# A graph network kernel: softmax sums rearranged by GpSimd's transfers, reciprocals of the different denominators only

## The reference

```
ex    = exp(leaky_relu(es[src] + ed[dst]) - max)      # first layer; exp(q.k / sqrt(32)) in the attention
alpha = ex / segment_sum(ex, dst)[dst]
out   = segment_sum(h[src] * alpha[:, :, None], dst)  # 8 heads of 32 columns
x1    = elu(out + b)                                  # first layer only
```

## Time and profile before

| | |
|---|---|
| median of 3 runs | 4061.83 us (4058.06 to 4066.59) |
| the profiled execution | 4059.45 us, its span 4057.7 us |
| first layer's loop, `stage_gat_aggregate` | about 742 to 1613 us of the span |
| attention's loop, `stage_attention` | about 2385 to 3489 us of the span |
| busy over the span | PE 77%, DVE 72%, ACT 56%, GpSimd 3% |
| bytes moved by DMA | 311 MB, mean 77 GB/s |

### The profile page before, as it was taken

How to read it: one execution, slowest core, us unless ns; L and a number is a source line. 1 busy time by engine, 2 the same in 40 slices (tenths; PEclk the granted TensorE clock), 3 DMA queues, 4 the chain that set the end, 5 groups by cost and what they waited for, 6 DMA issues and landing times. The chain is left out here.

```text
span 4057.7 us, 45830 instructions
## 1 busy us (share of the span) xinstructions
PE 3122.0 (77%) x15883; PEld 1597.5 (39%) x15885; DVE 2931.5 (72%) x3369; ACT 2292.0 (56%) x3244; POOL 140.2 (3%) x148
## 2 busy tenths in 40 slices
PE   3024766888888885899499489999999999589587
PEld 2012333322222221788467343333333333367454
DVE  4878987799999997355434649999999999611423
ACT  2000367899999997111133148989898989222032
POOL 0000000000000000000044100000000000000000
PEclk8556998999999998999699789999999999799599
DMA  1000134433333332443322412222222222200000
GB/s 45 0 0 0 71 131 162 123 98 97 98 97 95 97 98 58 150 156 127 121 61 65 151 56 78 76 77 76 76 76 77 76 78 76 77 22 0 14 3 32
DMA packets 178576, 311.21 MB, mean 77 GB/s; under 512 B 25648, under 2 KB 129054, under 8 KB 177880
## 3 DMA queue, kind: packets, MB, share of 16 engines
q1 hardware_dynamic: 172920, 293.84, 23.9%
q0 software_dynamic: 5472, 14.95, 1.2%
HBM read 247.26 MB, written 61.47 MB: 76 GB/s over the span
## 5 line engine op out<-in xcount | busy, mean ns | idle before, releaser
L891 PE MATMUL acc<-weights,messages 128*64 128x400 f32 x3200 | 624.6, 518 | 148.3 <-DVE weights L959 87.1
L2069 PE MATMUL acc<-weights,values 128*64 128x400 f32 x3200 | 639.2, 521 | 13.3 <-DVE weights L2179 9.3
L2176 DVE SCALAR_TENSOR_TENSOR weights<-x,counts 128x1600 f32<-128x1600 f32 x304 | 554.9, 1825 | 33.2 <-ACT x L2145 24.7
L2056 PE MATMUL scores<-q,k 32*128 32x400 f32 x3200 | 388.4, 555 | 71.5 <-ACT x L2140 65.3
L891 PEld LDWEIGHTS acc<-weights,messages 128*64 128x64 f32 x3200 | 202.1, 138 | 567.3 <-DVE weights L959 194.5
L2142 ACT ACTIVATE x<-scores 128x800 f32<-128x800 f32 x496 | 405.1, 838 | 17.2 <-PE scores L2056 17.2
L959 DVE SCALAR_TENSOR_TENSOR weights<-rho,kappa,counts 128x800 f32<-128x800 f32 x400 | 410.0, 1065 | 2.0 <-PE acc L891 2.0
L964 DVE TENSOR_TENSOR weights<-maxima,counts 128x1600 f32<-128x1600 f32 x200 | 363.6, 1818 | 42.4 <-ACT maxima L916 42.4
L911 ACT ACTIVATE maxima<-rho,wx 128x800 f32<-128x800 f32 x400 | 361.7, 952 | 34.6 <-DVE weights L964 30.2
L916 ACT ACTIVATE maxima<-maxima,kappa 128x800 f32<-128x800 f32 x400 | 360.0, 948 | 0.0
L2069 PEld LDWEIGHTS acc<-weights,values 128*64 128x64 f32 x3200 | 196.5, 137 | 407.3 <-issue 254.4
(11 more groups left out here) (311 smaller groups left out, 3647.9 us busy)
## 6 DMA issues: line engine op xcount, KB each, us to landing
counts<-edge_counts SPq DMA_DIRECT2D x200, 400.0 KB, 3.2
counts<-edge_counts SPq DMA_DIRECT2D x400, 200.0 KB, 2.4
edge_counts<-counts_out SPq DMA_DIRECT2D x40, 1000.0 KB, 4.2
counts<-edge_counts SPq DMA_DIRECT2D x25, 1600.0 KB, 7.6
w_first<-in_L_ffn_W_dram SPq DMA_DIRECT2D x8, 512.0 KB, 9.9
w_second<-in_L_ffn_W_dram SPq DMA_DIRECT2D x8, 512.0 KB, 9.6
normed_rows<-normed SPq DMA_DIRECT2D x5, 640.0 KB, 3.9
w_first<-expert_rows SPq DMA_DIRECT2D x5, 640.0 KB, 9.4
```

Source lines behind the costliest of these rows:

```text
L891: ins = nc.tensor.matmul(acc[64 * o:64 * o + 64, p, h, 0:CH], msg[:, t, r % 2 * Q + q, :], w[:, T % WR, q, half(h)], start=(t == 0), stop= ...
L2056: ins = nc.tensor.matmul(sc[:, (n + j // 2) % SR, j % 2, 0:CH], kT[part, r % KF, t * P:(t + 1) * P], q[part, r % 2, :], start=True, stop=True)
L2069: ins = nc.tensor.matmul(acc[64 * e:64 * e + 64, p, 0:CH], msg[:, t, r % KF * 2 + p, D * e:D * e + 2 * D], w[:, U % WR, 2 * p + e, :], sta ...
L2176: ins = nc.vector.scalar_tensor_tensor(out=w[:, U % WR, :, :], in0=out, scalar=EXP_HI, in1=counts, op0=ALU.min, op1=ALU.mult)
```

## The change

Both stages get the same new path, for every round:

- The 8 copies of `stack` on ACT are gone. GpSimd issues transfers instead (`spread_out`): 4 that write one of the 32 equal denominator rows of each head to DRAM, 4 that put the numerators of a head into their rows, and, after the first four have landed, 1 that reads the 4 rows of denominators back, spread over 128 partitions by 25 columns (first layer) or 64 by 25 (attention).
- DVE takes the reciprocal of that small tile only (`invert`; in the attention it is bounded first), behind tile 6 or tile 8 of the next round.
- GpSimd writes it to DRAM (1 transfer) and, after that has landed, reads it back with 4 transfers that repeat each row over 32 partitions (`bring_home`).
- DVE multiplies (`divide`), behind tile 11 or tile 16.
- In the first layer `elu_part` has 3 ACT instructions instead of 5; GpSimd does the other two with one tensor_scalar ahead of its addition.
- `copy_sums` waits for the transfers of the round before, and GpSimd for the tile that it overwrites; ACT no longer waits for that.

The attention's `spread_out` and `bring_home` are those of the first layer with its own offsets and are left out below, as are the lines that call the new functions after the last round.

```diff
 # stage_gat_aggregate
-    SUMS_AT, STACK_AT, DIVIDE_AT, ELU_AT = 0, 2, 10, 17
+    SUMS_AT, INVERT_AT, DIVIDE_AT, ELU_AT = 0, 6, 11, 13
+    SPREAD = CW * Q // P
...
+        spread = core.sb(ctx, "denominators_spread", [P, SPREAD])
+        den_dram = nc.dram_tensor("sums_of_weights", (2, ROUNDS, Q, CW), F32, kind="Internal").ap()
-        less = core.sb(ctx, "minus_one", [P, 1])
...
         def copy_sums(act, r):
+            if r:
+                act.wait_ge(s_raw, r * Q * 16)
+                act.wait_ge(s_stack, r * Q * 16)
             for p in range(2):
                 act.wait_ge(s_used, ((r + 1) * NT - 1) * USED_T + p + 1)
                 nc.scalar.copy(sums[:, p, :].rearrange("p (h n) -> p h n", h=2), acc[:, p, :, 0:CH]).then_inc(s_free, 1)
-            act.wait_ge(s_free, 2 * r + 2)
+
+        def spread_out(pool, r):
+
+            pool.wait_ge(s_free, 2 * r + 2)
+            for q in range(Q):
+                o = 64 * (q % 2) + D
+                pool.dma_start(den_dram[0, r, q:q + 1, :], sums[o:o + 1, q // 2, :]).then_inc(s_raw, 16)
             if r:
-                act.wait_ge(s_y, r)
-
-        def stack(m):
-
-            q = m % Q
-            o = 64 * (q % 2) + D * (m < Q)
-            to = den if m < Q else y
-            nc.scalar.copy(to[D * q:D * q + D, :], sums[o:o + D, q // 2, :]).then_inc(s_den, 1)
-
-        def divide(dve, m, r):
+                pool.wait_ge(s_y, r)
+            for q in range(Q):
+                o = 64 * (q % 2)
+                pool.dma_start(y[D * q:D * q + D, :], sums[o:o + D, q // 2, :]).then_inc(s_stack, 16)
+            pool.wait_ge(s_raw, (r + 1) * Q * 16)
+            pool.dma_start(spread[:, :], den_dram[0, r, :, :].rearrange("q (s n) -> (q s) n", n=SPREAD)).then_inc(s_spread, 16)
+
+        def bring_home(pool, r):
+
+            pool.wait_ge(s_inv, r + 1)
+            pool.dma_start(den_dram[1, r, :, :].rearrange("q (s n) -> (q s) n", n=SPREAD), spread[:, :]).then_inc(s_home, 16)
+            pool.wait_ge(s_home, (r + 1) * 16)
+            for q in range(Q):
+                pool.dma_start(den[D * q:D * q + D, :], den_dram[1, r, q, :].partition_broadcast(D)).then_inc(s_wide, 16)
+
+        def invert(dve, r):
+            dve.wait_ge(s_spread, (r + 1) * 16)
+            nc.vector.reciprocal(spread[:, :], spread[:, :]).then_inc(s_inv, 1)
+
+        def divide(dve, r):
+            dve.wait_ge(s_wide, (r + 1) * Q * 16)
+            dve.wait_ge(s_stack, (r + 1) * Q * 16)
+            nc.vector.tensor_tensor(y[:, :], y[:, :], den[:, :], ALU.mult).then_inc(s_div, 1)
+
+        def elu_part(act, m, r):
 
             if m == 0:
-                dve.wait_ge(s_den, (r + 1) * 2 * Q)
-            if m < 4:
-                part = den[:, m * (CW // 4):(m + 1) * (CW // 4)]
-                nc.vector.reciprocal(part, part).then_inc(s_div, 1)
-            else:
-                dve.wait_ge(s_div, r * 5 + 4)
-                nc.vector.tensor_tensor(y[:, :], y[:, :], den[:, :], ALU.mult).then_inc(s_div, 1)
-
-        def elu_part(act, m, r):
-
-            done = r * 5
-            if m == 0:
-                act.wait_ge(s_div, r * 5 + 5)
+                act.wait_ge(s_div, r + 1)
                 ins = nc.scalar.activation(y[:, :], y[:, :], ACT.Identity, bias=bcol[:, r % 2:r % 2 + 1])
             elif m == 1:
-                act.wait_ge(s_elu, done + 1)
+                act.wait_ge(s_elu, 3 * r + 1)
                 ins = nc.scalar.activation(ey[:, :], y[:, :], ACT.Relu, scale=-1.0)
-            elif m == 2:
-                act.wait_ge(s_elu, done + 2)
-                ins = nc.scalar.activation(y[:, :], y[:, :], ACT.Relu)
-            elif m == 3:
+            else:
+                act.wait_ge(s_elu, 3 * r + 2)
                 ins = nc.scalar.activation(ey[:, :], ey[:, :], ACT.Exp, scale=-1.0)
-            else:
-                act.wait_ge(s_elu, done + 3)
-                ins = nc.scalar.activation(y[:, :], y[:, :], ACT.Identity, bias=less[:, 0:1])
...
             @block.gpsimd
             def _(pool):
                 for r in range(ROUNDS):
-
-                    pool.wait_ge(s_elu, r * 5 + 5)
+                    spread_out(pool, r)
+                    bring_home(pool, r)
+
+                    pool.wait_ge(s_elu, 3 * r + 2)
+                    nc.gpsimd.tensor_scalar(y[:, :], y[:, :], 0.0, -1.0, ALU.max, ALU.add).then_inc(s_upper, 1)
+                    pool.wait_ge(s_upper, r + 1)
+                    pool.wait_ge(s_elu, 3 * r + 3)
                     nc.gpsimd.tensor_tensor(XT[:, r % 2, columns(r):columns(r) + CW], y[:, :], ey[:, :], ALU.add).then_inc(s_y, 1)
...
 # stage_attention
-    PROJECT_AT, SUMS_AT, STACK_AT, DIVIDE_AT = 14, 1, 2, 12
+    PROJECT_AT, SUMS_AT, INVERT_AT, DIVIDE_AT = 14, 1, 8, 16
+    PARTS = 64
+    SPREAD = Q * CH // PARTS
...
         def copy_sums(act, r):
 
             act.wait_ge(s_used, (r + 1) * NT)
+            if r:
+                act.wait_ge(s_raw, r * Q * 16)
+                act.wait_ge(s_stack, r * Q * 16)
             for p in range(2):
                 nc.scalar.copy(sums[:, p, :], acc[:, p, 0:CH]).then_inc(s_free, 1)
-            act.wait_ge(s_free, 2 * r + 2)
...
+        def invert(dve, r):
+
+            dve.wait_ge(s_spread, (r + 1) * 16)
+            nc.vector.tensor_scalar(spread[:, :], spread[:, :], 1e-20, None, ALU.max).then_inc(s_low, 1)
+            dve.wait_ge(s_low, r + 1)
+            nc.vector.reciprocal(spread[:, :], spread[:, :]).then_inc(s_inv, 1)
+
+        def divide(dve, r):
+
+            dve.wait_ge(s_wide, (r + 1) * Q * 16)
+            dve.wait_ge(s_stack, (r + 1) * Q * 16)
+            nc.vector.tensor_tensor(XT[:, r % KF, columns(r)], num, den, ALU.mult).then_inc(s_y, 1)
...
+                        if r and t == INVERT_AT:
+                            invert(dve, r - 1)
+                        if r and t == DIVIDE_AT:
+                            divide(dve, r - 1)
```

More of the change, by code:

```diff
@@ L945, in _ @@
             def _(dve):
-                nc.vector.memset(less[:, :], -1.0).then_inc(s_set, 1)
                 nc.vector.tensor_scalar(nkap[:, :, :], kap[:, :, :], -1.0, None, ALU.mult).then_inc(s_set, 1)
@@ L970, in _ @@
                             bound_rho(r + 1)
-                for m in range(5):
-                    divide(dve, m, ROUNDS - 1)
+                invert(dve, ROUNDS - 1)
+                divide(dve, ROUNDS - 1)
     core.stage_ends()
@@ L2088, in divide, with spread_out @@
-        def divide(dve, m, r):
-            if m == 0:
-                dve.wait_ge(s_den, (r + 1) * 2 * Q)
-                nc.vector.tensor_scalar(den, den, 1e-20, None, ALU.max).then_inc(s_div, 1)
-            elif m < 3:
-                dve.wait_ge(s_div, r * 3 + 1)
-                part = den[:, (m - 1) * (CH // 2):m * (CH // 2)]
-                nc.vector.reciprocal(part, part).then_inc(s_div, 1)
-            else:
-                dve.wait_ge(s_div, r * 3 + 3)
-                nc.vector.tensor_tensor(XT[:, r % KF, columns(r)], num, den, ALU.mult).then_inc(s_y, 1)
+        def spread_out(pool, r):
+            pool.wait_ge(s_free, 2 * r + 2)
+            for j in range(Q):
+                e = j % 2
+                o = 64 * e + D * (1 - e)
+                pool.dma_start(den_dram[0, r, j:j + 1, :], sums[o:o + 1, j // 2, :]).then_inc(s_raw, 16)
+            if r:
+                pool.wait_ge(s_y, r)
+            for j in range(Q):
+                e = j % 2
+                o = 64 * e + D * e
+                pool.dma_start(num[D * j:D * j + D, :], sums[o:o + D, j // 2, :]).then_inc(s_stack, 16)
+            pool.wait_ge(s_raw, (r + 1) * Q * 16)
+            pool.dma_start(spread[:, :], den_dram[0, r, :, :].rearrange("q (s n) -> (q s) n", n=SPREAD)).then_inc(s_spread, 16)
@@ L2149, in _ @@
                         copy_sums(act, r - 1)
-                    if r and 0 <= t - STACK_AT < 2 * Q:
-                        stack(t - STACK_AT)
                 copy_sums(act, ROUNDS - 1)
-                for m in range(2 * Q):
-                    stack(m)
+            @block.gpsimd
+            def _(pool):
+                for r in range(ROUNDS):
+                    spread_out(pool, r)
+                    bring_home(pool, r)
             @block.vector
@@ L2180, in _ @@
                     ins.then_inc(s_w, 1)
-                    if r and 0 <= t - DIVIDE_AT < 4:
-                        divide(dve, t - DIVIDE_AT, r - 1)
-                for m in range(4):
-                    divide(dve, m, ROUNDS - 1)
+                    if r and t == INVERT_AT:
+                        invert(dve, r - 1)
+                    if r and t == DIVIDE_AT:
+                        divide(dve, r - 1)
+                invert(dve, ROUNDS - 1)
+                divide(dve, ROUNDS - 1)
                 dve.wait_ge(s_y, ROUNDS)
```

37 lines of the change are left out of this document (19 added, 18 removed).

## The result

The changed kernel took **3942.12 us** (median of 4 runs, 3937.97 to 3943.77); the kernel before, run beside it, 4060.13. The ratio is 0.9705, with a 95% interval of 0.9688 to 0.9722. Forecast were 3969, with a range of 3935 to 4022. So the sign and the range held, and the gain is 118 us by the medians where 93 were forecast. The profiled execution is the 3937.97 one, with a span of 3936.2; against the span of before (4057.7) that is 121.5 us less, and this is what the traces have to account for.

The account below looks back on a forecast made before the run. DVE and ACT were near the span in the first layer, PE, DVE and ACT in the attention. Gains of 50 and 66 us less longer ends of 8 and 15 make 93: 3969 us, range 3935 to 4022.

Parts of the forecast that it names:

- the length of a round read from round 0: Both stages: round 0 has no sums to handle, so it shows a round's cost without the removed work.
- The attention's 63.4 us: Attention round after the change, set by PE: 25 tiles at 2.38 us (59.5), projection 1.5, waits 1.95 and 0.41.
- the two waits that were forecast to stay: Attention: PE waits 1.95 and 0.41 us a round where ACT stands behind the copy of sums; left in place.
- The attention's gain, forecast as 66: Attention: round falls from 67.8 to 63.4 us, 4.4 us a round over 15 rounds, 66 us.
- The sum said 100.0: First layer: DVE's terms make a round of 100.0 us, 7.2 us less each, 50 us over 7 rounds.
- DVE's idle: First layer, each round: DVE waits 2.0 us for PE's rows, 0.6 for ACT at tile 1, 0.5 for ACT's bunch.
- GpSimd's tensor_scalar: First layer: the new GpSimd instruction over 128x800 costs DVE 0.9 us a round, between nothing and above 1.7.
- Plus 8 and plus 15: After the last round, uncovered transfers lengthen the end: first layer 22.2 to 30.3 us, attention 9.0 to 24.0.
- An issue: GpSimd's queue, both stages: one direct transfer's issue priced at 1.0 us, between 0.33 and 1.25; 14 a round.
- The first (DVE held by descriptors): Attention: DVE's L2167 can't start while GpSimd issues, 3 us a round, 24 us less gain, 3993 us; chance 0.20.
- The second (transfers late): DVE's wait behind tile 8: transfers come late and the kernel is slower, 4120 us at 2.6 us an issue; chance 0.08.
- The third (only the first layer gains): PE already limits the attention, so only the first layer gains, 27 us, 4035 us; chance 0.06.

Follow-up runs that it names:

- `twice`: Changed kernel with every transfer of a group of four issued a second time into a scratch tensor, 26 issues a round instead of 14: 3950.22 us, ratio 0.9732.
- `elu_early`: Changed kernel with the first layer's old elu back (five ACT instructions) and the attention's `invert` behind tile 2 instead of 8: 3970.19 us, ratio 0.9778.
- `first_only`: Changed kernel with the attention put back as before, so only the first layer has the change: 4000.06 us, ratio 0.9854.
- `last_dve`: Changed kernel, last round of both stages with ACT copies and wide reciprocals, first layer's last tensor_scalar and addition on DVE: 3913.52 us, ratio 0.9637.

## Why the prediction was right, and where it was off

**Rounds, not shares.** The step that carried the forecast, the length of a round read from round 0, held. The attention's 63.4 us came out as 63.14: PE at 2.38 us a tile, and of the two waits that were forecast to stay (1.95 and 0.41) one of 1.81 did, which makes the 62.88 of most rounds. The slow matmuls of three rounds add 0.3 to the mean. That the forecast is so near is in part luck: a wait that went and a slowness that nobody had foreseen cancel. The attention's gain, forecast as 66, was 70.

**First layer, mis-sized by 21 us.** The sum said 100.0 and the round took 96.97. Two of its terms were too high:
- *DVE's idle.* 2.0 for PE's rows, 0.6 and 0.5 for ACT made 3.1 us a round. The groups show 4.4 us for PE and 4.8 for ACT over eight rounds; from the first to the last copies of sums, seven rounds, it is 2.4 and 3.3, which with 0.4 of other idle is 0.9 a round. The twice 0.97 of round 0 is there again after the change (0.97 and 1.00), but the seven later rounds share the other 2.4 us for PE. A wait of round 0 was taken for one of every round.
- *GpSimd's tensor_scalar.* It was priced at 0.9 on top of 1.7 for the addition. The timeline shows what the two take from DVE together:

```profile
893.60 4.44 POOL L950 TENSOR_SCALAR y<-y 128x800 f32<-128x800 f32 x1 [23.09 <-ACT denominators L864]
895.18 2.60 DVE L970 SCALAR_TENSOR_TENSOR weights<-rho,kappa,counts 128x800 f32<-128x800 f32 x2
...
899.93 3.16 DVE L970 SCALAR_TENSOR_TENSOR weights<-rho,kappa,counts 128x800 f32<-128x800 f32 x2 [0.41 <-PE acc L902]
```

  Two pairs of 2.60 and 3.16 us instead of 2.00 each are 1.76 us lost, as in all rounds but the last of the seven, where the addition alone had cost 1.66 and the sum had 2.6. The new instruction itself was not cheap, only not at DVE's cost: GpSimd took 4.4 us for it beside DVE and 2.88 alone, four times the 0.7 that the memset had suggested. The rule of the Trainium skill on two readers that exclude each other (SBUF — State Buffer, Who interferes with whom) agrees with the trace in kind: both GpSimd instructions stretch the DVE instruction with two SBUF inputs beside them. In size it doesn't: the pair that starts at 895.18 ends at 897.78, inside GpSimd's tensor_scalar (893.60 to 898.04), and loses 0.6 us; so DVE was not shut out for that instruction's length, as the prediction had read the rule. With the tensor_scalar DVE loses 0.1 us a round more than with the addition alone, and it was GpSimd that was stretched, by 1.5 and 1.3 us.

Together these make the 3.0 us (2.2 and 0.8). With 96.97 the earlier terms (25 tiles at 3.66, the bound of rho, a reciprocal of 0.3 us instead of 0.2, the product) stand as forecast.

**The ends, right by two errors.** Plus 8 and plus 15 were forecast, 23 in all; measured 10.0 and 11.0, 21. That these agree is luck: the visible part was over-priced and another part not seen. An issue took 0.50 us where 1.0 was taken, from the indirect transfer's 0.97: the price had been bounded by 0.33 and 1.25, and the true one was nearer to SP's. With 14 issues that is 7 us less at each end, and the landings were shorter too, so that the way out and home took 10 us less than forecast. The visible parts came out 7 and 10 us shorter (23.1 instead of 30.3, 14.0 instead of 24.0). In the first layer 2.4 of the 10 are lost again on a term that the sum of the tail had left out: GpSimd's own tensor_scalar, 2.88 us, only in part beside the last ACT instruction. And behind GpSimd's last instruction the changed kernel has 9.7 and 8.8 us before the next stage, of which no row of before showed anything, as both stages there had ended with 0.5. The prediction let the next stage begin where the last recorded instruction ends, and that step failed, by 9.2 and 6.0 us.

**The rivals.** The first (DVE held by descriptors) did not happen: 668 ns with 0, 14 and 26 issues a round. The second (transfers late) did not either: `twice` had no wait at `invert`. It is a real mechanism that needs the cover gone, as at tile 2 in `elu_early`. A slip in its sum changes nothing: two tails of 14 issues each grow by 28 us, not 26, for each us of their price. The third (only the first layer gains) was wrong; `first_only` shows the attention's half.

**In brief:** in the first layer the two halves of the change are worth more together than apart, since DVE and ACT were close to the same limit. Of what it frees, 21 us are given back at the ends of the two stages, and a last round of another form gets them back: the ends of `last_dve` are 16.7 and 7.3 us, 29.2 less than those of the changed kernel (32.7 and 20.5). Its span is 24.4 us shorter, as three more slow rounds in the attention take 4.9 back.

## What to carry to other kernels

Price a change by a round that lacks the work in question, and then test each idle term of that round in a later one: what fills a pipeline once is not paid each time. Work that is hidden in a loop is bare after its last round, so give the last round a version of its own: the fast path for the loop, the short path for the end. Where GpSimd issues many transfers in a stage, let its last instruction lie well ahead of the stage's end (28 us and more were enough here), and look at the silent time between the last recorded instruction and the next stage's first; no group of lines shows it.

## What was not expected of the hardware

- A stage in which GpSimd issued 14 transfers a round ended 8.5 to 9.7 us after GpSimd's last instruction, even where the last transfer was 81 us back; with 8 a round it was 5.7 and 11.1 us, with 26 a round 8.4 and 7.4; with one 512-byte transfer, or none, 0.5 us. What fills the time and sets its length stays open.
- A two-operation f32 tensor_scalar of 128x800 on GpSimd took 2.88 us alone, the addition of two tiles of that size 1.87; beside DVE 4.41 and 3.18.
- GpSimd issues a direct transfer in 0.50 us, whether of one row or of 32 rows of 3.2 KB (0.53 to 0.56 for the read-back), and in 1.1 where DVE's tensor_scalar of 128x1600 ran beside it, which took its usual 0.99; from SP's queue the last rounds' took 0.28 to 0.63.
- After a wait of 1.81 us PE ran at the lower clock for about 3 us in 3 of 15 rounds (granted clock 0.66 over 5 us, 0.50 over three of them, in the one shown), in 6 of 15 in two kernels with the same loop, and at the full clock in the others; where that wait was 1.10 us, no round was longer than the rest.
- GpSimd's tensor_scalar and DVE's instructions with two SBUF inputs ran side by side: a pair of DVE's finished inside it with 0.6 us lost, while GpSimd took 4.4 us instead of 2.9.
